# Cross-attention decoder on one core: the transposes of x1 go from TensorE to VectorE, and the jobs and SyncE's transfers around them change places

## What is computed

```python
x = _layernorm(x + self_attention(x, ...))       # the 16 x 16 heads of a short attention
x = _layernorm(x + cross_attention(x, ctx_1024, mask, Wq, Wk, Wv, Wo))
x = _layernorm(x + ffn(x, W_base, W_enc, W_dec, W_down, W_up, ...))

# cross attention, 16 heads of 16 dims, 512 queries against 1601 keys
scores = einsum('bhqd,bhkd->bhqk', q, k) / sqrt(16)
scores = where(mem_mask, scores, -inf)
out = einsum('bhqk,bhkd->bhqd', softmax(scores), v) @ Wo.T
```

## Time and profile before

| | |
|---|---|
| median of 3 runs | 1651.15 us (1650.35 to 1655.78) |
| the profiled execution's own time | 1650.58 us |
| its span, first to last instruction | 1648.8 us |
| TensorE matmul busy | 1586.7 us, 96% |
| VectorE busy | 1238.2 us, 75% |
| ScalarE busy | 1053.2 us, 64% |
| GpSimd busy | 161.2 us, 10% |
| granted TensorE clock, mean | 0.989 |

### The profile page before, as it was taken

The page is one execution under the profiler, slowest core; times in us unless marked ns, Lnnn a source line. Parts: engine busy times, 40 slices in busy tenths (PEclk is TensorE's granted clock), DMA queues, the critical chain, the costliest instruction groups (busy, mean ns, idle before and its releaser), DMA issues.

```text
span 1648.8 us, 25559 instructions
## 1 busy us (share of the span) xinstructions
PE 1586.7 (96%) x9632; PEld 588.7 (36%) x9632; DVE 1238.2 (75%) x1790; ACT 1053.2 (64%) x1998; POOL 161.2 (10%) x151
## 2 busy tenths in 40 slices
PE   6779999999999999999999999999999999999997
PEld 5442323332333333332333323433333323332233
DVE  5788777877788777887888777887778777887522
ACT  2227776676666666676666766676666776666661
POOL 7311000100011000100001000110001000000000
PEclk8899999999999999999999999999999999999999
DMA  5655071623517071442707163361707234150010
GB/s 156 116 143 101 25 138 41 101 69 86 96 40 127 28 131 40 90 93 62 116 22 134 32 113 69 69 112 52 121 12 122 61 52 77 50 78 5 11 33 16
DMA packets 118663, 125.22 MB, mean 76 GB/s; under 512 B 35186, under 2 KB 100339, under 8 KB 118540
## 3 DMA queue, kind: packets, MB, share of 16 engines
q1 hardware_dynamic: 117724, 123.06, 38.3%
q10 hardware_dynamic: 816, 0.53, 0.1%
HBM read 84.18 MB, written 35.03 MB: 72 GB/s over the span
## 4 chain that ended last, share of the span: by engine, by line
PE 85%; DVE 7%; ACT 3%; issue 3%; DMA 1%; SPq 0%; POOL 0%; POOLq 0%; DVEq 0%; ACTq 0%
PE banks L1122 23%; PE values L1141 23%; PE banks L1082 12%; PE work L1012 5%; PE work L998 5%; PE work L957 4%; DVE xneg_max_pieces L1439 4%; PE work L1019 3%; PE work L1025 3%; ACT xprobs L1260 3%; PE work L1004 2%; PE work L1028 1%; PE work L942 1%; PE work L1037 1%; DMA max_dram<-xneg_max_rows 1%
## 5 line engine op out<-in xcount | busy, mean ns | idle before, releaser
L1260 ACT ACTIVATE xprobs<-banks 128x512 f32<-128x512 f32 x1664 | 900.5, 595 | 408.3 <-PE banks L1122 405.0
L1439 DVE TENSOR_REDUCE xneg_max_pieces<-banks 128x2 f32<-128x1024 f32 x768 | 909.0, 1219 | 258.4 <-PE banks L1082 257.2
L1122 PE MATMUL banks<-xq_stacks,xk_stacks 99*128 99x512 bf16 (+1 forms) x1664 | 517.7, 385 | 9.9 <-ACT xprobs L1260 3.0
L1141 PE MATMUL values<-xprobs,xv_rows 128*17 128x512 f32 x3328 | 437.9, 598 | 1.3 <-ACT xprobs L1260 1.3
L1122 PEld LDWEIGHTS banks<-xq_stacks,xk_stacks 99*128 99x128 bf16 (+1 forms) x1664 | 127.4, 97 | 398.8 <-ACT xprobs L1260 273.2
L1082 PE MATMUL banks<-xk_stacks,xq_stacks 49*128 49x512 bf16 (+1 forms) x2048 | 250.3, 335 | 14.2 <-DVE xneg_max_pieces L1439 12.3
L1082 PEld LDWEIGHTS banks<-xk_stacks,xq_stacks 49*128 49x128 bf16 x2048 | 57.2, 94 | 327.6 <-DVE xneg_max_pieces L1439 212.9
L1510 POOL TENSOR_TENSOR xk_parts<-xk_rest,xk_parts 128x401 bf16<-128x401 f32 (+1 forms) x64 | 59.0, 923 | 660.5 <-ACT xk_parts L1239 660.5
L1141 PEld LDWEIGHTS values<-xprobs,xv_rows 128*17 128x17 f32 x3328 | 55.1, 95 | 122.9 <-issue 117.6
L1505 POOL TENSOR_TENSOR xrstd<-xrstd,mhalf 128x4 f32<-128x4 f32 x23 | 23.2, 1011 | 652.4 <-DVE xrstd L1314 652.4
L1012 PEld LDWEIGHTS work<-xvT,ctxT_a 128*128 128x128 f32 (+1 forms) x416 | 54.3, 192 | 13.6 <-issue 3.9
(11 more groups left out here) (295 smaller groups left out, 1007.3 us busy)
## 6 DMA issues: line engine op xcount, KB each, us to landing
xk_stacks<-key_parts_dram SPq DMA_DIRECT2D x186, 200.1 KB, 13.0
key_parts_dram<-xk_parts SPq DMA_DIRECT2D x144, 100.0 KB, 2.2
xq_stacks<-parts_dram SPq DMA_DIRECT2D x186, 64.0 KB, 8.8
ctxT_a<-in_ctxT SPq DMA_DIRECT2D x4, 1601.0 KB, 7.5
ctxT_b<-in_ctxT SPq DMA_DIRECT2D x4, 1601.0 KB, 7.5
parts_dram<-xq_parts SPq DMA_DIRECT2D x45, 128.0 KB, 2.0
key_parts_dram<-xk_parts SPq DMA_DIRECT2D x48, 100.2 KB, 5.2
xa<-in_x SPq DMA_DIRECT2D x8, 512.0 KB, 16.3
```

The source lines that it names most:

```text
L1122: pe.matmul(at, kst[0:ROWS[par], k, h2, par, t * P:(t + 1) * P], qst[0:ROWS[par], k, h2, par, :], start=True, stop=True).then_inc(made, 1)
L1141: last = pe.matmul(av[32 * j:32 * j + HD + 1, :], vals[:, k, t, gr * GH + j, :], probs[:, sl % 2, j, :], start=t == 0, stop=t == XKT - 1)
L1260: nc.scalar.activation(probs[:, sl % 2, j, :], score_bank(n)[0], ACT.Exp).then_inc(exped, 1)
L1439: nc.vector.tensor_reduce(nmp[:, of % 2, :, j2, q, piece], pairs[n % MRING][:, :, :], AX.X, ALU.max, negate=True).then_inc(on["mxr"], 1)
```

## The change

- The two `x1T` jobs of batches 1 to 7 are gone, with ScalarE's copy. VectorE makes `xT` with 16 instructions of a new step, `turn`. Each takes 32 partitions of `xa` and transposes eight blocks of 32x32 (256 elements per partition) into 32 partitions of `xT`. They stand at the ends of slots 13 to 22, one to three in a slot.
- Query job 0 goes from slots 12 and 13 to 23 and 24, so `v` 2, `enc`, `gram` move up, and `kproj` 4 goes from slot 22 to 25. `v` 3 becomes a job with a slot of its own (14), and `gram` 2 has two parts where it had three. `x2T` 1 goes from slot 16 to 15, `loss` and `choose` a slot earlier.
- `invert` and `scale` of group 1 go from slots 27 and 32 to 28 and 33.
- SyncE: query parts 0 come behind the maxima of group 2; the outputs of group 1 come before key part 4 and the context.

```diff
-        IN_BETWEEN = {
-            8: ("x1T", 0, NEXT), 11: ("x1T", 1, NEXT), 14: ("x2T", 0, PREV), 16: ("x2T", 1, PREV), 18: ("v", 3, NOW),
-            35: ("loss", 0, PREV),
-        }
+        IN_BETWEEN = {14: ("x2T", 0, PREV), 15: ("x2T", 1, PREV), 34: ("loss", 0, PREV)}
...
-            (("qproj", 0, NEXT), 2), (("v", 2, NOW), 2), (("enc", 0, PREV), 2), (("gram", 0, PREV), 2),
-            (("enc", 1, PREV), 2), (("kproj", 4, NEXT), 1), (("gram", 1, PREV), 2), (("enc", 2, PREV), 2),
-            (("gram", 2, PREV), 3), (("enc", 3, PREV), 2), (("gram", 3, PREV), 2), (("kproj", 5, NEXT), 1),
+            (("v", 2, NOW), 2), (("v", 3, NOW), 1), (("enc", 0, PREV), 2), (("gram", 0, PREV), 2),
+            (("enc", 1, PREV), 2), (("gram", 1, PREV), 2), (("qproj", 0, NEXT), 2), (("kproj", 4, NEXT), 1),
+            (("enc", 2, PREV), 2), (("gram", 2, PREV), 2), (("enc", 3, PREV), 2), (("gram", 3, PREV), 2),
...
+            13: turn_steps(0, 1), 14: [("invert", "o", 0, NOW), *turn_steps(1, 2)], 15: turn_steps(2, 3),
+            16: turn_steps(3, 5), 17: turn_steps(5, 7), 18: [("scale", "o", 0, NOW), *turn_steps(7, 8)],
+            19: turn_steps(8, 9), 20: turn_steps(9, 11), 21: turn_steps(11, 14), 22: turn_steps(14, N_TURNS),
+            28: [("invert", "o", 1, NOW)], 33: [("scale", "o", 1, NOW)],
...
+            elif name == "turn":
+                a, c = divmod(q, P // 32)
+                if q == 0:
+                    v.wait_ge(on["normed"]["x1"], b)
+                v.transpose(xT[32 * c:32 * (c + 1), :, :].rearrange("p k (n a i) -> p a k n i", a=P // 32, i=32)[:, a],
+                            xa[32 * a:32 * (a + 1), :, :].rearrange("p n (k c i) -> p c k n i", k=CH, i=32)[:, c]
+                            ).then_inc(x1_turned, 1)
...
             sp_move_outputs(m)
+            sp_spread_inverses(m)
+            sp_max_rows(m + 2)
             if nxt < B:
                 sp_query_parts(0, uses_before(0, nxt))
-            sp_spread_inverses(m)
-            sp_max_rows(m + 2)
+            sp_move_outputs(m + 1)
             if nxt < B:
                 sp_free_key_dram(nxt, 1)
                 sp_key_parts(4, use + 4)
                 if nxt + 1 < B:
                     sp_load_ctx(nxt + 1)
-            sp_move_outputs(m + 1)
-            if nxt < B:
                 sp_stacks(nxt, 0, m + 1)
```

More of the change, by code:

```diff
@@ L789, in cross_attention_and_ffn @@
         scaled = sem("x_outputs_scaled")
+        x1_turned = sem("x_x1_turned")
         x1_in = sem("x_x1_in")
@@ L838, in cross_attention_and_ffn @@
             (("xo", 0, PREV), 2), (("xo", 1, PREV), 2), (("kproj", 2, NEXT), 1), (("kproj", 3, NEXT), 1),
-            (("qproj", 0, NEXT), 2), (("v", 2, NOW), 2), (("enc", 0, PREV), 2), (("gram", 0, PREV), 2),
-            (("enc", 1, PREV), 2), (("kproj", 4, NEXT), 1), (("gram", 1, PREV), 2), (("enc", 2, PREV), 2),
-            (("gram", 2, PREV), 3), (("enc", 3, PREV), 2), (("gram", 3, PREV), 2), (("kproj", 5, NEXT), 1),
-            (("kproj", 6, NEXT), 1), (("kproj", 7, NEXT), 1), (("v", 4, NEXT), 2), (("v", 5, NEXT), 2),
-            (("mid", 0, PREV), 2), (("y", 0, PREV), 2), (("y", 1, PREV), 2), (("v", 6, NEXT), 2),
+            (("v", 2, NOW), 2), (("v", 3, NOW), 1), (("enc", 0, PREV), 2), (("gram", 0, PREV), 2),
+            (("enc", 1, PREV), 2), (("gram", 1, PREV), 2), (("qproj", 0, NEXT), 2), (("kproj", 4, NEXT), 1),
+            (("enc", 2, PREV), 2), (("gram", 2, PREV), 2), (("enc", 3, PREV), 2), (("gram", 3, PREV), 2),
+            (("kproj", 5, NEXT), 1), (("kproj", 6, NEXT), 1), (("kproj", 7, NEXT), 1), (("v", 4, NEXT), 2),
+            (("v", 5, NEXT), 2), (("mid", 0, PREV), 2), (("y", 0, PREV), 2), (("y", 1, PREV), 2), (("v", 6, NEXT), 2),
             (("qproj", 1, NEXT), 2), (("v", 7, NEXT), 1),
@@ L854, in norm_steps, with turn_steps @@
             return [(step, what, q, rel) for q in range(first, last)]
+        N_TURNS = (P // 32) ** 2
+        def turn_steps(first, last):
+            return [("turn", "x1", n, NEXT) for n in range(first, last)]
         def choose_steps(first, last):
@@ L860, in cross_attention_and_ffn @@
             1: [("invert", "o", 3, PREV)], 4: [("aggr", "x1", 0, NEXT)],
-            14: [("invert", "o", 0, NOW)], 18: [("scale", "o", 0, NOW)],
-            27: [("invert", "o", 1, NOW)], 32: [("scale", "o", 1, NOW)],
+            13: turn_steps(0, 1), 14: [("invert", "o", 0, NOW), *turn_steps(1, 2)], 15: turn_steps(2, 3),
+            16: turn_steps(3, 5), 17: turn_steps(5, 7), 18: [("scale", "o", 0, NOW), *turn_steps(7, 8)],
+            19: turn_steps(8, 9), 20: turn_steps(9, 11), 21: turn_steps(11, 14), 22: turn_steps(14, N_TURNS),
+            28: [("invert", "o", 1, NOW)], 33: [("scale", "o", 1, NOW)],
             40: [("invert", "o", 2, NOW)], 44: [("scale", "o", 2, NOW)],
             2: norm_steps("stats", "x1", 0, 2, NEXT), 3: norm_steps("stats", "x1", 2, 4, NEXT),
-            5: [*norm_steps("apply", "x1", 0, 2, NEXT), ("scale", "o", 3, PREV)],
+            5: [("scale", "o", 3, PREV), *norm_steps("apply", "x1", 0, 2, NEXT)],
             6: norm_steps("apply", "x1", 2, 4, NEXT), 8: norm_steps("stats", "x2", 0, 2, PREV),
@@ L868, in cross_attention_and_ffn @@
             11: norm_steps("apply", "x2", 0, 2, PREV), 12: norm_steps("apply", "x2", 2, 4, PREV),
-            35: choose_steps(0, 4), 36: choose_steps(4, 8), 37: choose_steps(8, CHOOSE_STEPS),
+            34: choose_steps(0, 4), 35: choose_steps(4, 8), 36: choose_steps(8, CHOOSE_STEPS),
             45: norm_steps("stats", "y", 0, 2, PREV), 47: norm_steps("stats", "y", 2, 4, PREV),
@@ L1001, in pe_job @@
                 if part == 0 and not ph.first:
-                    pe.wait_ge(on["w_free"], ph.order.after(("x1T", 1, b)))
+                    pe.wait_ge(x1_turned, N_TURNS * b)
                 for kin in units(part, parts, CH):
@@ L1545, in sp_load_x @@
                 nc.sync.wait_ge(on["x1_out"], 16 * (b - 1))
-                nc.sync.wait_ge(on["w_free"], MAIN.order.after(("x1T", 1, b - 1)))
+                nc.sync.wait_ge(x1_turned, N_TURNS * (b - 1))
             nc.sync.dma_start(xa[:], g.x[b].rearrange("(q p) d -> p q d", p=P)).then_inc(on["x_in"], 16)
```

## The result

The changed kernel takes **1673.77 us** in the median of five runs (1659.42 to 1679.27), the kernel before 1651.15 in the same comparison: a ratio of 1.0119, with a 95% interval of 1.0087 to 1.0151. It is slower by 1.2%, where 1647 us was forecast and "faster" was the likeliest outcome. A second comparison on another chip gave 1663.83 us (1654.26 to 1665.72) against 1650.5, ratio 1.0073 [1.0052, 1.0094]. So the sign is certain and the size is not: one run of the changed kernel differs from another by up to 20 us, while 23 runs of the kernel before lay between 1647 and 1657.

What follows compares the result with a forecast made beforehand. The prediction took TensorE, 85% of the chain, to bound the kernel. From 1650.6 us it subtracted a gain of 12.4 and added a loss of 8.4, giving 1646.6, stated as 1647 us, with a range from 1638 to 1658.

Steps and rivals of the forecast that it cites:

- The gain: Time saved by removed transposes and rearranged jobs, less a charge for VectorE's transposes, over all batches: 12.4 us.
- The loss: Time lost through SyncE's new order and the DMAs, as waits for late stacks, maxima and inversion: 8.4 us.
- The transposes taken from TensorE: Slots 8 and 11 shorten without `x1T`, by 0.66 and 0.89 us, together 1.55 us in each of batches 1 to 6.
- VectorE's transposes: 16 per batch at 0.42 us each, nearly all in VectorE's idle time in slots 13 to 23; charged 0.1 us a batch.
- The rearranged jobs: `v` 3 in its own slot and `gram` 2 in two parts save 0.29 us a batch; other jobs only change places.
- D: Delay of the key stacks and everything behind, from the context load ahead of them: 4.4 us, bounds 1.3 and 7.3.
- rival 3: Stacks later still, D 5.5 to 7, batches 1 to 5 also waiting at slot 39: 1655 to 1663 us, chance 0.09.
- What D costs: Batch 0 loses 4.4 us, batches 1 to 5 together 3 at slot 39 and 1 for the later inversion at slot 40.
- a margin of 3.8 to 4.9 us: Time by which group 3's maxima precede TensorE at slot 39: 3.8 us in batch 1, 4.9 in batch 3.
- Rival 1: The cover holds, D is under 2.5 us and only batch 0 loses, up to 2: 1638 to 1641 us, chance 0.22.
- Rival 2: VectorE becomes the bound, a transpose taking 0.67 us, so slots 16 to 22 overrun: 1657 us, chance 0.10.
- Rival 4: Unseen waits in jobs that follow closely in slots 14 and 15 make the gain smaller: 1650 us, chance 0.09.

Runs made afterwards that it cites:

- x_later: Changed kernel with the store of x1 and the loads of x and its attention moved behind the maxima, context left in place: 1653.45 us.
- both runs on transposes: Changed kernel with the context loaded early, and each VectorE transpose either made twice (1691.31 us) or cut to an eighth (1646.16 us).
- again: The changed kernel measured once more, unaltered: 1663.83 us, ratio 1.0073.
- outputs_last: Changed kernel with the outputs of group 1 put back behind key part 4 and the context: 1653.14 us, ratio 1.001.
- before_ctx_late: Kernel before with only the context load moved behind the outputs of group 1, ahead of the stacks: 1665.62 us, ratio 1.0107.
- turns_twice: Changed kernel with the context loaded early, and each of VectorE's 16 transposes of a batch made twice: 1691.31 us, ratio 1.0259.
- ctx_early: Changed kernel with the context load moved right behind the inverses of group 0: 1646.79 us, ratio 0.9969.
- ctx_x_later: Changed kernel with both moves, context right behind the inverses of group 0 and x loads and stores behind the maxima: 1641.89 us, ratio 0.9952.

## Why the prediction was wrong

The gain was nearly right: by the loop, 10.4 us (kernel before against both moves in the changed kernel) where 12.4 were forecast. The loss was not: 20.7 and 17.5 us in the loops of the two traces of the changed kernel, each the fastest run of its comparison, against that same kernel with both moves, where 8.4 were forecast. The steps in turn:

- **The transposes taken from TensorE: right.** 0.66 and 0.89 us a batch were forecast for slots 8 and 11; 0.66 and 0.88 measured.
- **VectorE's transposes: right.** The 112 of them take 422 to 442 ns, 0.42 was taken:

```profile
L1335 DVE STREAM_TRANSPOSE xT<-xa x112: 422/436/442, 170.0 to 1337.0; 32x256 f32<-32x256 f32 x112
```

  Nothing waits for them in the changed kernel. The rule of the Trainium skill ("VectorE: DVE Perf Modes", Rules for kernel authors) that a 128x128 transpose belongs on TensorE would have left the jobs where they were. Here the runs disagree with it: slots 8 and 11 give 1.54 us a batch, against 0.08 for the longer transposes on VectorE, and with SyncE in order the move and its job table gain 5 to 10 us. No run separates the two, but the reason fits the traces: TensorE is full and VectorE has gaps. The doubled transposes show how narrow the ground is.
- **The rearranged jobs: wrong by 0.7 us a batch, half of it offset.** The step said that `v` 3 in a slot of its own costs about 2.9 us, and slot 14 with `x2T` near 3.5. It took 4.03:

```profile
733.17 1.05 PE L1146 MATMUL values<-xprobs,xv_rows 128*17 128x512 f32 x8
734.19 0.66 PE L947 MATMUL work<-ident,x 128*128 128x128 f32 x4
...
735.76 0.60 PE L1017 MATMUL work<-xvT,ctxT_b 128*65 128x128 f32 x4
...
737.20 1.05 PE L1146 MATMUL values<-xprobs,xv_rows 128*17 128x512 f32 x8
```

  Four matmuls of 65 rows take 0.60 us, so they fill a slot as half a job does: 3.41, and 0.6 for `x2T`. The saving of 0.29 is a loss of 0.2 (3.41 + 4.22 + 3.41 against 10.81), and slots 12 to 51 together are 0.45 us longer than before, 0.08 of it for the transposes. Against it stands a gain that I didn't see, 0.35 us in slots 6 and 7 (3.92 and 3.41 before, 3.41 and 3.57 after): the scaling of group 3 now runs ahead of the normalising of x1, so the output projection no longer waits for it. (That is an edit of `VECTOR_WORK` in slot 5 which the list of changes doesn't name.) In sum a batch without waits went from 189.01 to 187.59, a gain of 1.42 where 1.74 was forecast. The last batch, which was to gain 0.5, loses 0.2.
- **D, the lateness of the key stacks: mis-sized, and the first to fail.** It was put at 4.4 us and is 5.2 to 6.5, inside the bounds of 1.3 to 7.3 and near the 5.5 to 7 of rival 3. In batch 3 the context goes out 1.6 us after the outputs' end, not 1.3. Of the 5.3 us there, 1.4 is the write going out later (10.4 us after the start of slot 26, before 8.9) and 3.9 its longer way. It goes out when the query stacks are issued, and the later inversion, which was put at nothing, would not let it go before 10.2. The sum let the small write be 1.6 us behind the landing of the context at 7.3 us. The load landed after 7.7 us beside the query stacks (8.1 and 8.4 in the page's medians), and the write 1.8 us behind it. The row that I used for the load was of a time when it had the engines to itself. The ring order that the Trainium skill describes ("DMA: Bandwidth & Descriptors", Queues, rings and completion order) agrees with this trace: 5.6 us for 8 KB.
- **What D costs: the step that made the sign wrong.** I charged batches 1 to 5 only what D exceeds a margin of 3.8 to 4.9 us by. With the measured D that rule gives 1.7 us in batch 1 and 0.4 in batch 3 at slot 39; the trace has 2.75 and 2.67. Four things were missing. First, the delay does not pass on unchanged: D was 5.3 us at the key stacks of batch 3, but the maxima were read 7.8 us later, in batch 1 6.9. There the margin of 3.8 to 4.9 us and a wait of 2.7 to 2.8 add up to the delay within 0.4 us. Why it grows there and shrinks to 2.5 in batch 4 is open; x stands in it, since x_later takes 3.7 us off in batch 3. Second, slot 13: I looked at the deadlines behind the stacks of slot 26, not at the other maxima, whose first scores come 1.9 us sooner because slots 6, 8 and 11 had become shorter. A store of x1 stands in their way, and slot 12, where TensorE waits for them, is 0.1, 0.2 and 1.8 us longer in batches 3, 4 and 6. Third, the clock: at the two longest waits TensorE fell to 1.2 GHz for 6.8 and 3.4 us. By the slots that adds 3.0 us in batch 0 and 1.6 in batch 1 to 7.0 us of waits. Fourth, scatter: a landing time that used to vary under cover now varies on the path, so the median run is 14 us above the best one. The profile before has no row for the last two. By batches, batch 0 loses 8.4 us (4.4 forecast), batches 1 to 5 lose 10.6 together (3 forecast, and 1 for what lies behind) and batch 6, which loads no context, 1.7.
- **The rivals.** Rival 1 is excluded by the waits. Rival 2 needed 0.67 us a transpose and is excluded by 0.436 and by both runs on transposes. Rival 3 had the mechanism, its place and nearly D right, at a chance of 0.09, and its 1655 to 1663 us holds the profiled execution (1659.4), but neither that of the second comparison (1654.3) nor the medians of 1673.8 and 1663.8. Its sign that slot 35 waits in batches 1 to 5 did not show. Rival 4 named the right place, slots 14 and 15, but what costs there is work, the four matmuls of `v` 3, and not a wait.
- **The weight of the step.** That SyncE's order costs was forecast, and so was where. The choice of 4.4 between 1.3 and 7.3 stood on one row, against a margin of 3.8 to 4.9. With D as measured and the rule unchanged the loss is, by my estimate from these margins, 12 to 15 us (6.5 in batch 0, 4 to 7 in batches 1 to 5, 1 behind), and the time about that of before: that the kernel is slower took the rule's failure too. The chance of "slower" should have been that of D above the margin, not 0.19.

Still open: how the 14 us between the best run and the median divide among places. No run separates the later inversion, the moved query parts or the new order in slot 5 from the rest of the change either.

## What to carry to other kernels

A large load in a queue is paid by the small transfers issued behind it, and here by their whole round trip: ask, for every DMA of a megabyte that is moved, which write of a few KB is next and who waits for its return. The margin to a deadline must be compared with the upper end of the delay, not with its likeliest value, since beyond it waits come in many batches, scatter, and can bring the lower clock with them. A delay at one transfer need not be the delay at the next: here 5.3 us became 7.8. And where an edit shortens slots, look at every deadline that comes nearer, also those whose transfers it doesn't touch.

## What the runs showed of the hardware

- TensorE's granted clock fell to 0.50 near the end of waits of 4.25 us (for 6.8 us) and 2.75 us (for 3.4 us) in the changed kernel, 3.02 in again (3.4), 3.26 in outputs_last and 2.91 in x_later (6.8 each), and 2.24 in before_ctx_late and 2.19 in turns_twice (3.4 each). It stayed at 1.00 at waits of 2.67 (changed kernel, batch 3), 2.95 (again, batch 2), 2.03 (outputs_last) and 1.9 (ctx_early). So the length of one wait does not tell in these traces whether the clock falls. In batch 3 of turns_twice it fell at the second of two waits of 1.33 and 1.72 us.
- A float32 transpose of VectorE takes 436 ns for 256 elements on 32 partitions, and 202 ns for 32, about as long as the bf16 one of 32 elements:

```profile
L1335 DVE STREAM_TRANSPOSE xT<-xa 32x32 f32<-32x32 f32 x112 | 22.6, 202 | 3.3
```

  That is (436 - 202) / 224 = 1.04 ns an element and 0.17 us besides. The Trainium skill ("Vector Engine (DVE) Microarchitecture Reference", The reshape front-end and per-opcode configuration) has the transpose sustain one element per cycle and lane. The slope fits that if a cycle is 1.04 ns, which no run here shows.
- The same 8 KB write of the maxima was back after 2.0, 3.9, 6.6, 6.9 or 10.6 us in batch 3 of ctx_x_later, the kernel before, ctx_early, x_later and the changed kernel. What differs is the order of what was issued before it, and in the kernel before the tables too.
